# Repeated loads moved from SyncE's queue to ScalarE's, and a longer ring of three buffer pairs, in a normalise-and-gate kernel

## What is computed

```python
xn = group_norm(x)                       # 32 groups of 16 channels, per batch, no affine
xl1 = bn_relu(dwconv(xn, w1), g1, b1)    # w1: (C,1,256,1): sum over rows,    result (b, c, 1, 256)
xl2 = bn_relu(dwconv(xn, w2), g2, b2)    # w2: (C,1,1,256): sum over columns, result (b, c, 256, 1)
dot = einsum('bck,bck->cb', xl1[:, :, 0, :], xl2[:, :, :, 0])
num = dot.reshape(b, c)                  # the (c, b) array is read as (b, c)
num = (num @ lw1.T + lb1) @ lw2.T + lb2
num = softmax(num, axis=1)
out = x + xn * num[:, :, None, None]
```

## Time and profile before

| | |
|---|---|
| median of three runs | 1786.57 us |
| profiled execution | 1788.11 us, span 1786.4 us |
| HBM read and written | 458.82 MB, 268.44 MB |
| busy share of the span: PE, DVE, ACT, POOL | 27%, 52%, 36%, 18% |
| mean rate of the transfers | 408 GB/s |
| mean granted TensorE clock | 0.633 |

### The profile page before, as it was taken

One profiled execution on the slowest core, in us unless ns is written; L12 is line 12 of the kernel. 1 busy time (PEld: TensorE's weight loads), 2 busy tenths in 40 slices (PEclk: granted clock), 3 DMA queues, 4 the chain that ended last, 5 costly groups with the idle time before them and its releaser, 6 DMA issues.

```text
span 1786.4 us, 12512 instructions
## 1 busy us (share of the span) xinstructions
PE 484.8 (27%) x3214; PEld 163.5 (9%) x3214; DVE 933.8 (52%) x4046; ACT 649.6 (36%) x504; POOL 318.1 (18%) x409
## 2 busy tenths in 40 slices
PE   4588566642132322322322233440000000000000
PEld 1132122120000010100100010120000000000000
DVE  5899699933655654555565546963222222222221
ACT  4688587844444544543355345510000000000000
POOL 7678587820000000000000000010000000000000
PEclk8899788865666656656665666765555555555555
DMA  9997899959999999999999999999999999999999
GB/s 387 425 427 304 356 427 427 427 223 419 403 428 401 405 411 409 400 394 430 404 398 405 399 400 431 429 369 413 430 433 430 432 431 431 431 431 431 431 430 409
DMA packets 52425, 728.07 MB, mean 408 GB/s; under 512 B 6273, under 2 KB 6785, under 8 KB 8066
## 3 DMA queue, kind: packets, MB, share of 16 engines
q1 hardware_dynamic: 34210, 463.03, 61.7%
q10 hardware_dynamic: 18144, 264.25, 35.2%
HBM read 458.82 MB, written 268.44 MB: 407 GB/s over the span
## 4 chain that ended last, share of the span: by engine, by line
DMA 53%; another core or an unknown queue 26%; ACT 7%; DVE 6%; PE 4%; SPq 1%; issue 1%; POOL 1%; ACTq 0%; POOLq 0%; DVEq 0%
DMA xs<-in_x 40%; DMA out<-xs 12%; DVE mul_junk L829 4%; ACT sq_junk L650 4%; ACT xs L711 3%; PE ps_part L478 2%; DVE xs L907 1%; DMA z<-in_w 1%; SPq L307 1%; PE ps_l L571 0%; PE ps_m L584 0%; PE ps_l L559 0%; SPq L263 0%; SPq L255 0%
## 5 line engine op out<-in xcount | busy, mean ns | idle before, releaser
L829 DVE SCALAR_TENSOR_TENSOR mul_junk<-xs,ps_w 128x256 bf16<-128x256 f32 x1856 | 643.1, 417 | 317.3 <-DMA xs<-in_x 290.4
L650 ACT ACTIVATE sq_junk<-xs 128x4096 fp8e5<-128x4096 f32 x128 | 463.3, 3619 | 421.7 <-DMA xs<-in_x 405.9
L478 PE MATMUL ps_part<-xs,taps 128*32 128x512 f32 x2048 | 339.8, 824 | 658.2 <-DMA xs<-in_x 658.2
L907 DVE TENSOR_SCALAR xs<-xs,scale,shift 128x4096 f32<-128x4096 f32 x98 | 239.9, 2467 | 409.8 <-DMA xs<-in_x 409.2
L478 PEld LDWEIGHTS ps_part<-xs,taps 128*32 128x32 f32 x2048 | 91.0, 144 | 879.8 <-issue 866.0
L829 DVE DVE_READ_ACCUMULATOR mul_junk<-xs,ps_w 128x1 f32 x1856 | 153.3, 83 | 0.0
L396 POOL TENSOR_TENSOR rstd_b<-var,minus_half 128x2 f32<-128x2 f32 (+1 forms) x16 | 12.4, 774 | 717.8 <-DVE var L856 717.8
L370 POOL TENSOR_TENSOR prod<-xs,w_copy 128x768 f32<-128x768 f32 x64 | 116.4, 1825 | 79.8 <-DMA xs<-in_x 77.5
L711 ACT ACTIVATE xs<-xs,shift,scale 128x4096 f32<-128x4096 f32 x30 | 113.7, 3788 | 14.0 <-DVE scale L940 7.1
L376 POOL TENSOR_TENSOR prod<-prod 128x384 f32<-128x384 f32 x64 | 63.0, 1006 | 0.0
L380 POOL TENSOR_TENSOR prod<-prod 128x192 f32<-128x192 f32 x64 | 36.6, 594 | 0.0
(11 more groups left out here) (100 smaller groups left out, 280.6 us busy)
## 6 DMA issues: line engine op xcount, KB each, us to landing
xs<-in_x SPq DMA_DIRECT2D x216, 2048.0 KB, 19.8
out<-xs ACTq DMA_DIRECT2D x126, 2048.0 KB, 27.1
xs<-in_lw SPq DMA_DIRECT2D x2, 2048.0 KB, 20.8
out<-xs SPq DMA_DIRECT2D x2, 2048.0 KB, 10.9
w_c<-in_w_rows SPq DMA_DIRECT2D x1, 512.0 KB, 4.6
w_sb<-in_w SPq DMA_DIRECT2D x1, 512.0 KB, 9.7
z<-in_w SPq DMA_DIRECT2D x1, 512.0 KB, 23.7
affine_in<-in_g SPq DMA_DIRECT2D x2, 16.0 KB
```

Of the source, the lines that this page charges most:

```text
L478: last = nc.tensor.matmul(ps_part[g % 2][32 * a:32 * a + 32, :], taps[:, g // QG % 2, g % 2, hf * JH + j, :], xs[:, s[0]:s[1] + 1:s[1] - s ...
L650: nc.scalar.activation(sq_junk[:], xs[:, s, :], ACT.Square, accum_out=sq_sum[:, u % 2, u // 2, b:b + 1], saturate=False).then_inc(squared, 1)
L829: last = nc.vector.scalar_tensor_tensor(out=mul_junk[:, sets[0] % 2, j - first, :], in0=xs[:, s, j * W:(j + 1) * W], scalar=1.0, in1=ps_w2 ...
L907: return nc.vector.tensor_scalar(xs[:, s, :], xs[:, s, :], scale[:, b, g:g + 1], shift[:, b, g:g + 1], ALU.mult, ALU.add)
```

## The change

Two things are changed. `RING3` is raised from 15 to 19, so that units 15 to 18 use the three pairs of slots, too. And the repeated loads from number 2 on are issued by ScalarE: after it has issued the store of rework r it waits until the store of rework r − 1 is complete, and issues repeated load r + 1. SyncE issues repeated loads 0 and 1 alone.

```diff
-RING3 = 15
+RING3 = 19
...
             def load_again(r):
                 s = rework_slot(r)
-                if r < 2:
-                    free_of_statistics(FIRST - 2 + r, 1)
-                else:
-                    sp.wait_ge(x_stored[s], written(s, ("re", r - 2)))
+                free_of_statistics(FIRST - 2 + r, 1)
                 sp.dma_start(xs[:, s, :], x_v[r // 2, :, 0, part_of(r)]).then_inc(x_loaded[s], 16)
...
                 load(u, 0)
                 if u >= FIRST + 2:
                     load(u, 1)
-                if u - FIRST + 2 < REWORK:
-                    load_again(u - FIRST + 2)
...
                 scaled_by_act(s, r // 2, reworked, r + 1)
                 store(r, 0, s)
+                n = r + 1
+                if 2 <= n < REWORK:
+                    t = rework_slot(n)
+                    act.wait_ge(x_stored[t], written(t, ("re", n - 2)))
+                    act.dma_start(xs[:, t, :], x_v[n // 2, :, 0, part_of(n)]).then_inc(x_loaded[t], 16)
```

## The result

The changed kernel takes 1794.85 us (median of 7 runs, 1791.41 to 1798.99) against 1787.03 of the kernel before on the same chip (7 runs): 1.0039 times, 95% interval 1.0026 to 1.0052. It is slower by 7 to 8 us where 20 us less were forecast. The profiled execution took 1792.27 us, span 1790.5.

What follows compares the result with a forecast made beforehand. Transfers set the time. From 1788.1 us, 15 for the first hole and 6 for the middle loop were taken off: 1767, kept at 1767 after a 1.5 us lower median and unit 20's risk; range 1752 to 1789.

Steps and rivals of the forecast that it cites:

- Part 1, gain 15 us: First stretch: with three pairs until unit 19 the hole at 165 to 190 goes; last unit-31 load at 344.4, not 359.90.
- a hole at 215 to 225: Sign against the first-stretch gain; its opposite was no slice under 400 GB/s between 134 and 223 us.
- The wait at the start of the middle, 2 us: At 394 to 450, the third repeated load waits for store 0; ACT stands some 8 us, 2 us charged.
- The form of the loop: Middle, two units from T: store T+3.85, next repeated load issued T+4.3, landed 19.6, first-row store landed 26.4.
- The join: In the middle loop, a queue joining one already running gets its share only 3.3 us after its issue.
- Data end 48.5, landed T+50.5 ... Idle 1.5 us ... the period is 51.2 us: Loop's end: SyncE's backlog lasts until 53.7, ACT's next store data starts at 55.2; period 51.2 us against 51.6 before.
- without a gap: In the middle loop, the two first-row stores, issued by T+17, follow the repeated load in ACT's queue with no pause.
- They are lost when both queues drain together: Middle loop before the change: the 2.9 us lost per period of 51.6 us fall where both queues run dry.
- Rival A: Middle: the reload chain on ACT becomes the bound, a joining queue getting its half at once; period 53.6, 1795 us; 19%.
- Both signs that were to prove it: Middle: a period over 53 and a rate under 400 GB/s would prove that the reload chain on ACT is the bound.
- The point from which it decides, a period of 52.9: Middle loop: from a period of 52.9 on, the reload chain on ACT decides against the change.
- The rule that each DMA engine takes turns between the queues that have work: Both DMA queues: turns go packet by packet; the earlier trace agreed once both run, not at a join.

Runs made afterwards that it cites:

- late_reload_sp_sq: Kernel before with RING3 = 19, repeated loads on SyncE one place later, and the unit's statistics ahead of its rework on ScalarE: 1754.47 us, 0.9813.

## Why the prediction was wrong, step by step

- *Part 1, gain 15 us*: right. 15.7 us alone; the softmax's last step came at 374.99 instead of 391.48. Unit 20 was the tight place, and the sign that I had named for a failure, a hole at 215 to 225, is there in part, as is slice 5 with 395 GB/s, under the 400 of the same sign (table by stretch):

```profile
215.00:220.00 5.00, 1.48 (x10) 0.30 (x2) 5.00 (x31) 3.84 (x3) 5.00 (x7) 1.00 0.63 223
```

  It cost next to nothing in the landings: the load of unit 20 was issued at 215.97 and landed 11.78 us later, at 227.75; the last load of the first stretch landed at 345.1 (forecast 344.4).
- *The wait at the start of the middle, 2 us*: right. 378 to 450 runs at 415 GB/s, a loss of 2.7 us.
- *The form of the loop*: right up to the last landing. From T = 701.51 the store was issued at T+3.85 (forecast 3.85), the next repeated load landed at T+19.56 (19.6). The join held too: SyncE's load was issued at 728.39, T+26.9 (26.4), and in the three microseconds from then, ScalarE's queue alone moved data; the view has no line for q1 (DMA view, 728.4 to 731.4 us):

```profile
q10 hardware_dynamic: 79, 1.29, 101.9%
q14 instruction: 2, 0.02, 1.3%
```

- *"Data end 48.5, landed T+50.5 ... Idle 1.5 us ... the period is 51.2 us"*: this step failed. The load landed at T+53.1 and the period was 53.3. The mechanism, ScalarE's scaling between landing and next issue under a backlog of SyncE, was the one that the sum used; its sizes were too small, and two of them depend on each other. First, the sum let ScalarE's queue pass from transfer to transfer "without a gap", and the two places above, from T+6.5 to T+10.5 and from T+17.5 to T+22.5, lose 0.6 and 1.0 us. From T+29.9 to the landing that queue still moved 4.57 MB (DMA view, 731.4 to 754.6), where the sum had 9.4 us of work, 4.05 MB:

```profile
q1 hardware_dynamic: 361, 5.39, 54.3%
q10 hardware_dynamic: 327, 4.57, 46.1%
```

  At half rate the 0.52 MB more take 2.4 us (an estimate from this one loop), nearly all of the 2.6 by which the landing is late. Second, SyncE's backlog dates from its issue at T+26.9 and doesn't wait, so a later landing finds less of it, and the drain that follows is deeper: 2.9 us in the mean instead of 1.5. In all a loop lost 4.6 us over its transfers where the sum had 2.5. Twelve loops times 2.1 us are 25 us, and the miss was 27.9.
- *"They are lost when both queues drain together"*, said of the loop before: not all of it. A place like the second one, just behind a drain, stands in the kernel before as well, 5 us after the store's issue at 592.22, with the loads behind it in the other queue (table by stretch), and loses 0.8 us in 1.5:

```profile
597.00:598.50 1.50, 1.50 (x12) 0.41 (x8) 1.50 (x11) 1.03 (x2) 0.00 (x0) 0.50 0.88 213
```

  This row could have told of it, and the sum for the loop after has no term for it.
- *Rival A*: its price, 1795, is what was measured, and so is its period, 53.6 for 53.3. Both signs that were to prove it came, a period over 53 and under 400 GB/s in the middle. They didn't tell A's reason from a deeper drain: A needed a queue that gets its half at once, and the join at 728.39 shows that it doesn't. So the agreement with its number is in part luck. The point from which it decides, a period of 52.9, was right, and only 1.7 us from the forecast one. A loop that repeats twelve times multiplies each microsecond that a hand-made sum leaves out, and 19% for A was too little with a backlog of 5.2 us against 6.7 to be covered.
- *The rule that each DMA engine takes turns between the queues that have work* (the Trainium skill, DMA: Bandwidth & Descriptors, "Queues, rings and completion order"): the trace after agrees as the one before did with even turns once both run (732 to 740 us: 1.84 MB of q1, 1.59 of q10), and not with them for some 3 us after an issue (728.4 to 731.4: none of q1).

## What to carry to other kernels

When a transfer's issue is moved to an engine that also computes on what it loads, write down the loop landing, computing, issue, landing: it is a cycle, and whatever computing lies in it must be covered by transfers already queued elsewhere. Moving the wait off one in-order stream does not remove it; first try another place in the same stream, and work that frees buffers ahead of work that waits. Two parts of a change with effects of opposite sign are to be measured apart: here −16 and +23 us looked like +7.

## What the runs showed of the hardware

- After a drain, the end of the first transfer costs rate although the next was issued microseconds before: 238 to 320 GB/s for 2 us where a load stands behind the store in the same queue, 0.6 us in each of eleven loops (with the two microseconds ahead of it counted in), and 213 GB/s for 1.5 us before the change, where the loads stand in the other queue. In `late_reload_sp_sq`, with the loads in one queue and the stores in the other, eleven slices of the middle run at 430 GB/s. Whether the change between store and load or the drain before it is the cause, no run here separates.
- A queue with a new transfer got nothing for the first 3 us while the other was full, in the kernel after (728.4 to 731.4), and next to nothing before.
- A thin stretch in the mean rate need not delay a landing: 190 to 220 us ran at 381 GB/s instead of 431, and from the last load of unit 14 (landed 170.99) to that of unit 31 (345.10) a transfer landed every 5.12 us, where the sum took 5.08 from an undisturbed stretch. That the slowest of the DMA engines sets them is a reading; the views here give the mean of the engines only.
